# A transformer block with a routed self-attention on one core: work moved from VectorE to ScalarE, and orders redone around the routed attention and at the opening

## The chip, the cores and the metric

One NeuronCore of a Trainium2 chip runs the program; the other cores are not used. The metric is the device time of one execution in microseconds. The kernel before was timed three times: 2812.5, 2813.47 and 2815.11 us, median 2813.47.

## The reference

64 batches of x (256 tokens, 256 channels) and of a context (77 keys, 192 channels), fp32. First a cross-attention with 8 heads of 64, then a routed ("expert") self-attention with 16 experts; both with a layer norm in front and a residual.

```python
x = x + xattn(layernorm(x), ctx)          # q = x Wq, k = ctx Wk, v = ctx Wv, softmax, Wo, + bo
x = x + ffn(layernorm(x))

def ffn(h):
    logits = normalize(h) @ normalize(sim) - sigmoid(gates)     # 256 tokens x 16 experts
    mask = logits > 0, or the 2 best where none is
    rw = softmax(where(mask, relu(logits), -inf))
    q, k, v = [einsum("te,ted->td", rw, einsum("tc,ecd->ted", h, p)) for p in (q_proj, k_proj, v_proj)]
    a = softmax(causal(q k^T / 8)) v                            # one head of 64
    return einsum("ted,edc->tc", a[:, None, :] * rw[:, :, None], o_proj)
```

## The kernel before, in words

Each fp32 product is done as three products of a high and a low part (fp32r tiles `_hi` and `_lo`): `product` issues them in lines 467, 468 and 469. So whatever TensorE is to read is written twice: ScalarE evacuates the hi part from PSUM or SBUF, then VectorE the lo part as source minus hi.

The cross-attention is folded: for each group of three batches, "jobs" compute keys (`k`), values (`v`), and from them gq (key times Wq, 8 jobs `g`) and uo (value times Wo, 8 jobs `u`). These are written to DRAM through a two-slot buffer `draft` by SP and loaded back per batch, `gq` (1232 KB) by `load_g` and `uo` (1024 + 208 KB) by `load_u`. A batch then goes through these stages:

- A: `ln1_a` (statistics of x), the power on GpSimd, `ln1_b` (normalise to xn), `a_xT` (transpose), `a_s` (scores, four quarters, with the maxima L1163 on VectorE), `a_exp` (L893, 16 exponentials on ScalarE), `a_psum`, `a_p` (L1506, the softmax product on GpSimd), `a_pT` (transposes in three parts), `a_y` (product with uo; evacuation L1185 adds the residual and gives x2).
- B: `ln2_a`, power, `ln2_b` (x2n), `b_norm`, `b_xT` (L632), `b_qkv` 0 to 15: projections of 8 pairs of experts by 2 token tiles; `b_qkv(n, j)` has pair j // 2 and tile j % 2. Pair 0 brings the router's logits along; from these `b_top` and `b_index` on VectorE, `b_route_1`, `b_route_2`, `b_w` on GpSimd, `b_exp` on ScalarE, `b_wsum` on VectorE and `b_rw` on GpSimd (L1482) make the weights rw. Then VectorE evacuates every projection: pair 0 as `acc = bank * rw` (L1232, "opening"), the others as `acc += bank * rw` (L1235). `b_sum` on GpSimd (L1491) adds the two experts of a pair.
- C: `c_qk` (transpose q and k; four ScalarE and two VectorE pieces), `c_s` (scores, L666), `c_exp`, `c_p`, `c_pT`, `c_pv`, `c_mix` (attention times rw per expert, L1276, then L961 on ScalarE and L1511 on GpSimd), `c_y` (output product), store.

All engines run the same list of steps i = -2 to 65, each with an order written out by hand. In step i, `nxt` is batch i + 2 (ln1, a_xT), `ahead` batch i + 1 (rest of A), `now` batch i (ln2, b_xT, b_qkv 0 to 5), `before` batch i - 1 (b_qkv 6 to 15, then C up to the mix), `earlier` batch i - 2 (c_y). Between them stand the slots E0 to E3, M1 to M3, L1, L2, in which `turn` runs a key or value job. `JOBS[i % 3]` says which: kind 0 has g3 to g7, k3, v0, v1; kind 1 has u0 to u5, v2, v3 and ct (context transpose); kind 2 has u6 (E0), u7 (E1), k0, k1, g0, g1, k2, g2. In kind 2, SP also issues four context loads at the step's start, and `load_u` of the next batch right after the u7 store in E1; otherwise `load_u` stands behind M3. `load_x(i + 2)` and `load_g(i + 2)` stand behind E0's store on SP.

An engine executes its list in order, so a wait holds everything behind it. The projections go round three PSUM banks: `ring_b` (L505 to L513) makes fill f wait until fill f - 3 is evacuated, so `b_xT`'s second part waits for `b_qkv` 14 of the batch before. The cross-attention shares three other banks in the order `A_ORDER`; `freed` makes a slot wait for the last holder.

The opening: weights are loaded in 16 pieces through three staging areas and split into hi and lo (`split_weights`), at places that `SPLIT_AFTER` names; the first group's jobs run one after another. Pieces 6 to 13 are the expert projections, 14 and 15 o_proj.

## Time and profile before

| | |
|---|---|
| median of 3 runs | 2813.47 us |
| the profiled execution | 2814.86 us |
| its span, first to last instruction | 2813.1 us |
| mean granted TensorE clock, of full speed | 0.978 |
| busy: TensorE (matmul), VectorE, ScalarE, GpSimd | 90%, 78%, 49%, 39% |
| chain that ended last: TensorE, VectorE, ScalarE, issue, DMA | 59%, 19%, 12%, 7%, 2% |
| DMA queues: SP's (q1), ScalarE's (q10) | 374.15 MB, 68.17 MB |
| L1235 on VectorE, the later projection evacuations | x1792, 410 ns each, 659.7 us |
| L1276 on VectorE, the mix | x256, 906 ns each, 231.8 us |
| L1436 on GpSimd, the powers (two forms) | x128, 871 ns each, 111.4 us |
| L1136 on VectorE, keys and values lo | x352, 395 ns each, 139.2 us |

Busy times are unions of an engine's instructions. Matmuls are pipelined: one lasts 0.28 to 0.36 us by the profile, while the next starts 0.12 to 0.18 us later, so idle time before a matmul is a little shorter than what the wait cost. "Issue" is time in which the engine waited for nothing that the profile shows.

### The profile page before, as it was taken

Reading aid. Unit: us, or ns where it says so; the run is one execution under the profiler, and the core shown is the slowest. Engines: PE = TensorE matmul, PEld = TensorE weight load, DVE = VectorE, ACT = ScalarE, POOL = GpSimd, SP = SyncE. Lnnn points to the kernel's source line nnn. Section 1 sums busy time; section 2 is a strip of 40 time slices with the busy share of each in tenths; the row PEclk is TensorE's granted clock in tenths of the full one; section 3 lists DMA queues with packets and bytes.
Section 4 is the critical chain, followed back from the end, with each engine's and each line's share of the span. In section 5 each row is a group of like instructions: output and inputs, shape, how many; then the busy total and the mean of one; then the engine's idle time right before and its main releaser. Section 6 shows DMA issues by size and latency. Waiting matters only on the chain.

```text
span 2813.1 us, 53794 instructions
## 1 busy us (share of the span) xinstructions
PE 2528.2 (90%) x17308; PEld 2427.3 (86%) x17308; DVE 2201.7 (78%) x6491; ACT 1378.8 (49%) x4598; POOL 1103.9 (39%) x1611
## 2 busy tenths in 40 slices
PE   4599999999999899999999999999989999999987
PEld 3589889889889889889889989988989988988986
DVE  5488888888888777878878878888778888888874
ACT  4454454555455454455455545545445455545531
POOL 0134344434434434434434434433434433443442
PEclk6699999999999999999999999999999999999998
DMA  7555555464555455455555555465555446455531
GB/s 188 186 158 169 172 165 160 139 189 142 172 170 161 149 165 164 137 184 154 168 163 169 155 157 177 133 186 155 169 159 163 156 146 189 139 173 167 161 91 41
DMA packets 299936, 445.75 MB, mean 158 GB/s; under 512 B 36857, under 2 KB 210873, under 8 KB 291465
## 3 DMA queue, kind: packets, MB, share of 16 engines
q1 hardware_dynamic: 230024, 374.15, 41.5%
q10 hardware_dynamic: 69632, 68.17, 10.9%
q8 instruction: 140, 2.29, 0.3%
q14 instruction: 140, 1.14, 0.1%
HBM read 257.91 MB, written 184.35 MB: 157 GB/s over the span
## 4 chain that ended last, share of the span: by engine, by line
PE 59%; DVE 19%; ACT 12%; issue 7%; DMA 2%; POOL 1%; SPq 0%; DVEq 0%; ACTq 0%; POOLq 0%
PE bank_b L467 9%; PE bank_b L469 8%; PE bank_b L468 8%; DVE acc L1235 5%; PE bank_a L467 4%; PE bank_c L467 4%; PE bank_c L469 4%; PE bank_c L468 4%; PE bank_a L468 4%; PE bank_a L469 4%; DVE both L1136 2%; DVE pT_lo L1179 2%; DVE probs L1081 2%; ACT both L852 1%; ACT both L851 1%
## 5 line engine op out<-in xcount | busy, mean ns | idle before, releaser
L467 PE MATMUL bank_b<-wqkv_hi,x2T_lo 128*128 128x384 f32 (+1 forms) x2048 | 724.7, 354 | 18.4 <-DVE acc L1232 18.1
L1235 DVE SCALAR_TENSOR_TENSOR acc<-bank_b,rw,acc 128x192 f32<-128x192 f32 x1792 | 659.7, 410 | 61.5 <-PE bank_b L469 54.9
L469 PE MATMUL bank_b<-wqkv_hi,x2T_hi 128*128 128x384 f32 (+1 forms) x2048 | 692.2, 338 | 0.0
L468 PE MATMUL bank_b<-wqkv_lo,x2T_hi 128*128 128x384 f32 (+1 forms) x2048 | 690.8, 337 | 0.0
L1511 POOL TENSOR_TENSOR mixs_lo<-mix,mixs_hi 128x512 fp32r<-128x512 f32 x256 | 404.1, 1609 | 227.0 <-ACT mixs_hi L961 227.0
L893 ACT ACTIVATE probs<-bank_a,s_max 128x77 f32<-128x77 f32 x1024 | 317.3, 330 | 281.8 <-DVE s_max L1163 279.2
L467 PEld LDWEIGHTS bank_b<-wqkv_hi,x2T_lo 128*128 128x128 f32 x2048 | 386.6, 189 | 29.5 <-DVE acc L1232 26.8
L468 PEld LDWEIGHTS bank_b<-wqkv_lo,x2T_hi 128*128 128x128 f32 x2048 | 387.9, 189 | 0.0
L469 PEld LDWEIGHTS bank_b<-wqkv_hi,x2T_hi 128*128 128x128 f32 x2048 | 384.6, 188 | 0.0
L1506 POOL TENSOR_TENSOR probs<-probs,p_sum 128x616 f32<-128x616 f32 x128 | 155.8, 1217 | 356.9 <-DVE p_sum L1170 356.9
L467 PE MATMUL bank_c<-wo_hi,mixs_lo 128*128 128x256 f32 x1024 | 288.6, 282 | 3.7 <-POOL mixs_lo L1511 3.7
L1436 POOL TENSOR_TENSOR pow_out<-pow_in,expo 128x2 f32<-128x2 f32 (+1 forms) x128 | 111.4, 871 | 452.2 <-DVE pow_in L1073 315.9
L469 PE MATMUL bank_c<-wo_hi,mixs_hi 128*128 128x256 f32 x1024 | 288.1, 281 | 0.0
L468 PE MATMUL bank_c<-wo_lo,mixs_hi 128*128 128x256 f32 x1024 | 287.7, 281 | 0.0
L961 ACT ACTIVATE mixs_hi<-mix 128x512 fp32r<-128x512 f32 x256 | 161.7, 632 | 231.4 <-DVE mix L1276 231.4
L1136 DVE TENSOR_TENSOR both<-bank_a,only 64x231 fp32r<-64x231 f32 x352 | 139.2, 395 | 141.3 <-ACT both L852 139.0
L1276 DVE TENSOR_TENSOR mix<-rw_all,late_tiles 128x512 f32<-128x512 f32 x256 | 231.8, 906 | 2.2 <-ACT late_tiles L957 2.1
L893 ACT ACTIVATION_READ_ACCUMULATOR probs<-bank_a,s_max 128x1 f32 x1024 | 215.4, 210 | 0.0
L467 PE MATMUL bank_a<-uo,pT_lo 128*128 128x256 f32 (+1 forms) x640 | 189.2, 296 | 18.1 <-issue 17.9
L467 PEld LDWEIGHTS bank_c<-wo_hi,mixs_lo 128*128 128x128 f32 x1024 | 193.4, 189 | 4.1 <-issue 3.8
L468 PEld LDWEIGHTS bank_c<-wo_lo,mixs_hi 128*128 128x128 f32 x1024 | 194.2, 190 | 0.0
L469 PEld LDWEIGHTS bank_c<-wo_hi,mixs_hi 128*128 128x128 f32 x1024 | 193.5, 189 | 0.0
(204 smaller groups left out, 6161.7 us busy)
## 6 DMA issues: line engine op xcount, KB each, us to landing
g_dram<-draft SPq DMA_DIRECT2D x176, 462.0 KB
gq<-g_dram SPq DMA_DIRECT2D x64, 1232.0 KB, 5.5
uo<-u_dram SPq DMA_DIRECT2D x64, 1024.0 KB
rw_all<-rw_dram ACTq DMA_DIRECT2D x128, 512.0 KB, 7.4
u_dram<-draft SPq DMA_DIRECT2D x176, 308.0 KB
xt<-in_x_dram SPq DMA_DIRECT2D x64, 256.0 KB, 3.9
out_dram<-mix SPq DMA_DIRECT2D x64, 256.0 KB, 6.2
u_dram<-draft SPq DMA_DIRECT2D x88, 156.0 KB
```

The lines of the kernel that those rows point to most:

```text
L467: nc.tensor.matmul(dst, lhs[1], rhs[0], start=start, stop=False)
L468: nc.tensor.matmul(dst, lhs[0], rhs[1], start=False, stop=False)
L469: return nc.tensor.matmul(dst, lhs[0], rhs[0], start=False, stop=stop)
L893: last = nc.scalar.activation(probs[:, t, h * NC:(h + 1) * NC], bank_a(f"S{j}")[:, k * NC:(k + 1) * NC], ACT.Exp, bias=s_max[:, j, k:k + 1 ...
L961: nc.scalar.activation(mixs[0][:, 2 * j:2 * j + 2, :], mix[:, 2 * j:2 * j + 2, :], copy).then_inc(mix_hi, 1)
L1081: V.tensor_scalar(dst[:, t, :], src[:, t, :], mv[k][:, t, 0:1], pow_out[k][:, 0, t:t + 1], ALU.subtract, ALU.mult).then_inc(ln_done[k], 1)
L1136: last = V.tensor_tensor(both[rows, k, e, cols], src[rows, cols], only.bitcast(F32)[rows, k, e, cols], ALU.subtract)
L1235: V.scalar_tensor_tensor(acc[:, t, k, :], src, rw[:, t, e:e + 1], acc[:, t, k, :], ALU.mult, ALU.add).then_inc(b_evac, 1)
L1276: V.tensor_tensor(mix[:, 2 * j:2 * j + 2, :], rw_all[:, 2 * j:2 * j + 2, :], aT2[:, :].unsqueeze(1).to_broadcast([P, 2, T]), ALU.mult).the ...
L1436: G.tensor_tensor(dst, src, expo[:, 0:m], ALU.pow).then_inc(ln_pow[k], 1)
L1506: G.tensor_tensor(part, part, p_sum[:, half, 1, :, :].unsqueeze(3).to_broadcast([P, NT, HB, NC]), ALU.mult).then_inc(p_ready, 1)
L1511: G.tensor_tensor(mixs[1][:, 2 * j:2 * j + 2, :], mix[:, 2 * j:2 * j + 2, :], mixs[0].bitcast(F32)[:, 2 * j:2 * j + 2, :], ALU.subtract).t ...
```

## The change

- The projections' opening pieces (pair 0, both tiles) go from VectorE to ScalarE: `b_first(n, t)`, two scaled copies each, after a wait for rw. TensorE's and VectorE's waits follow with a semaphore of their own, `acc_opened`, and `b_read`'s count shrinks.
- `ln1_b` and `ln2_b` go from VectorE to ScalarE, as `Identity` with a scale and a bias. VectorE makes the negated mean (`minus`), GpSimd multiplies it with the power's result (`shift`).
- VectorE: ln1_a moves from E2 to E0, between `b_norm` 0 and 1; ln2_a behind the first maximum; `b_qkv` 12 ahead of the E2 job, 15 ahead of E3; `c_qk` ahead of the M2 job; `b_index` ahead of `c_s`; `b_wsum` and `a_y` ahead of `c_pT`; `b_qkv` 2 and 3 ahead of the mix.
- ScalarE: `c_qk` ahead of the M2 job.
- TensorE: `b_qkv` 2 ahead of `c_s`, `a_y` whole ahead of `c_pT`, `b_qkv` 3 ahead of `c_pv`.
- Opening: SP issues the first `load_g` and `load_u` before the steps; weight pieces 11 to 15 are split within step -1, and 14 and 15 loaded there; the first `ln1_b` stands on ScalarE behind the query weights.

```diff
@@ -88,7 +88,8 @@
     def b_read(n, fill):
-        return (B_QKV + 2 * NT * EP) * n + (fill + 1 if fill < B_QKV else 2 * fill)
+        assert not B_QKV <= fill < B_QKV + NT
+        return (B_QKV + 2 * NT * (EP - 1)) * n + (fill + 1 if fill < B_QKV else 2 * (fill - NT))
 
@@ -334,7 +339,7 @@
         SPLIT_AFTER = {("k", 1): (W_V,), ("k", 2): (W_O - 1, W_O), ("k", 3): (6,), ("v", 0): (7,), ("v", 1): (8,),
-                       ("u", 0): (9,), ("u", 2): (10,), ("u", 7): range(11, len(PIECES))}
+                       ("u", 0): (9,), ("u", 2): (10,)}
 
@@ -430,10 +435,14 @@
                     load_x(i + 2)
-                if on(i + 2):
+                if i == -1:
+                    load_weights((14,))
+                if on(i + 2) and i + 2 > 0:
                     load_g(i + 2)
+                if i == -1:
+                    load_weights((15,))
                 turn("E1")
-                if i % 3 == 2 and on(i + 1):
+                if i % 3 == 2 and on(i + 1) and i + 1 > 0:
                     load_u(i + 1)
@@ -451,10 +460,12 @@
                 load_weights(pieces)
-            for hc, pieces in enumerate(((12,), (13,), (), (14, 15))):
+            load_g(0)
+            for hc, pieces in enumerate(((12,), (13,), (), ())):
                 store_u(0, 2 * hc)
...
                 load_weights(pieces)
+            load_u(0)
             for i in range(-2, B + 2):
@@ -507,7 +518,9 @@
                 if n or fill >= B_BANKS:
-                    if fill >= B_BANKS:
+                    if B_QKV <= fill - B_BANKS < B_QKV + NT:
+                        pe.wait_ge(acc_opened, at(NT, n, fill - B_BANKS - B_QKV))
+                    elif fill >= B_BANKS:
                         pe.wait_ge(b_evac, b_read(n, fill - B_BANKS))
@@ -794,13 +807,13 @@
                 do(now, b_qkv, 1)
+                do(now, b_qkv, 2)
                 do(before, c_s)
-                do(now, b_qkv, 2)
                 fill("Y", ahead, a_y, 0)
+                do(ahead, a_y, 1)
                 do(before, c_pT)
-                do(ahead, a_y, 1)
+                do(now, b_qkv, 3)
                 do(before, c_pv)
-                do(now, b_qkv, 3)
                 do(now, b_qkv, 4)
@@ -912,6 +925,37 @@
 
+            def b_first(n, t):
+                act.wait_ge(rw_ready, at(1, n, 0))
+                act.wait_ge(b_fill, b_at(n, B_QKV + t))
+                if n == 0:
+                    act.wait_ge(sim_step, 5)
+                else:
+                    act.wait_ge(qkv_ready, at(NT, n - 1, t))
+                for e in range(2):
+                    last = nc.scalar.activation(acc[:, t, e, :], bank_b(B_QKV + t)[:, E + e * QKV:E + (e + 1) * QKV], copy,
+                                                scale=rw[:, t, e:e + 1])
+                last.then_inc(acc_opened, 1)
+
+            def ln_b(k, n, src, dst):
+                act.wait_ge(ln_shift[k], at(1, n, 0))
+                for t in range(NT):
+                    nc.scalar.activation(dst[:, t, :], src[:, t, :], ACT.Identity, bias=shift[k][:, t:t + 1],
+                                         scale=pow_out[k][:, 0, t:t + 1]).then_inc(ln_done[k], 1)
+
+            def ln1_b(n):
+                if n:
+                    act.wait_ge(xt_fill, at(1, n - 1, 0))
+                    act.wait_ge(pt_fill, at(3, n - 1, 2))
+                ln_b(0, n, xt, xn)
+
+            def ln2_b(n):
+                if n:
+                    act.wait_ge(b_fill, b_at(n - 1, B_XT + 1))
+                if n > 1:
+                    act.wait_ge(mix_lo, at(4, n - 2, 1))
+                ln_b(1, n, x2_tiles[n % 3], x2n)
+
             def c_part(n, fill, dst, src):
@@ -965,6 +1009,7 @@
                     query_weights()
+                    ln1_b(0)
                 elif kind == "k":
@@ -999,27 +1044,42 @@
                 do(before, c_rT)
+                if i == -1:
+                    split_weights(11)
                 do(ahead, a_exp, 0)
...
                 do(ahead, a_exp, 3)
+                if i == -1:
+                    split_weights(12)
+                do(now, ln2_b)
                 turn("E1")
...
                 do(ahead, a_pT, 2)
+                if i == -1:
+                    split_weights(13)
+                if nxt:
+                    do(nxt, ln1_b)
                 turn("E3")
...
                 do(nxt, a_xT)
+                if i == -1:
+                    split_weights(14)
+                do(before, c_qk)
                 turn("M2")
-                do(before, c_qk)
                 turn("M3")
+                if i == -1:
+                    split_weights(15)
                 do(before, c_exp)
                 do(now, b_exp)
+                do(now, b_first, 0)
                 do(before, c_pT)
+                do(now, b_first, 1)
                 do(before, c_pv)
@@ -1069,41 +1129,26 @@
                 dve.wait_ge(ln_stats[k], at(2 * NT, n, 2 * NT - 1))
+                if n:
+                    dve.wait_ge(ln_shift[k], at(1, n - 1, 0))
+                V.tensor_scalar(minus[k][:, :], mv[k][:, :, 0], -1.0, None, ALU.mult).then_inc(ln_var[k], 1)
                 if k == 0:
...
 
-            def ln_b(k, n, src, dst):
-                dve.wait_ge(ln_pow[k], at(1, n, 0))
-                for t in range(NT):
-                    V.tensor_scalar(dst[:, t, :], src[:, t, :], mv[k][:, t, 0:1], pow_out[k][:, 0, t:t + 1],
-                                    ALU.subtract, ALU.mult).then_inc(ln_done[k], 1)
-
...
             def b_norm(n, k):
                 if k == 0:
+                    dve.wait_ge(ln_pow[1], at(1, n, 0))
                     V.tensor_tensor(rn[:, 0, :], pow_out[1][:, 0, :], pow_out[1][:, 1, :], ALU.mult).then_inc(rn_step, 1)
@@ -1220,20 +1265,15 @@
                 dve.wait_ge(b_fill, b_at(n, fill))
-                if j == 0:
-                    dve.wait_ge(rw_ready, at(1, n, 0))
-                if ep == 0 and n:
-                    dve.wait_ge(qkv_ready, at(NT, n - 1, t))
                 for k in range(2):
                     e = 2 * ep + k
-                    lo = (E if ep == 0 else 0) + k * QKV
-                    src = bank_b(fill)[:, lo:lo + QKV]
-                    if ep == 0:
-                        V.tensor_scalar(acc[:, t, k, :], src, rw[:, t, e:e + 1], None, ALU.mult).then_inc(b_evac, 1)
+                    src = bank_b(fill)[:, k * QKV:(k + 1) * QKV]
+                    if ep == 1:
+                        dve.wait_ge(acc_opened, at(NT, n, t))
                     else:
                         dve.wait_ge(b_evac, b_read(n, fill - NT) - 1 + k)
-                        V.scalar_tensor_tensor(acc[:, t, k, :], src, rw[:, t, e:e + 1], acc[:, t, k, :],
-                                               ALU.mult, ALU.add).then_inc(b_evac, 1)
+                    V.scalar_tensor_tensor(acc[:, t, k, :], src, rw[:, t, e:e + 1], acc[:, t, k, :],
+                                           ALU.mult, ALU.add).then_inc(b_evac, 1)
 
@@ -1285,7 +1325,7 @@
                 def do(n, fn, *k):
-                    if on(n) and not (fn in (ln1_a, ln1_b) and n == 0):
+                    if on(n) and not (fn is ln1_a and n == 0):
                         fn(n, *k)
@@ -1305,56 +1345,62 @@
                 do(before, b_qkv, 7)
+                if i == -1:
+                    split_weights(11)
+                do(ahead, a_s, 0)
                 do(now, ln2_a)
-                do(ahead, a_s, 0)
                 do(before, b_qkv, 8)
                 do(ahead, a_s, 1)
-                do(now, ln2_b)
                 do(before, b_qkv, 9)
                 do(ahead, a_s, 2)
-                do(now, b_norm, 0)
                 do(before, b_qkv, 10)
-                do(now, b_norm, 1)
                 do(ahead, a_psum, 0)
                 do(ahead, a_s, 3)
+                do(now, b_norm, 0)
+                do(nxt, ln1_a)
+                do(now, b_norm, 1)
+                do(ahead, a_psum, 1)
                 do(now, b_norm, 2)
-                do(ahead, a_psum, 1)
                 do(before, b_qkv, 11)
+                if i == -1:
+                    split_weights(12)
                 turn("E1")
                 do(earlier, c_y)
+                do(before, b_qkv, 12)
                 turn("E2")
-                do(nxt, ln1_a)
-                do(before, b_qkv, 12)
                 do(ahead, a_pT, 0)
...
                 do(ahead, a_pT, 2)
-                do(nxt, ln1_b)
+                if i == -1:
+                    split_weights(13)
                 do(before, b_qkv, 14)
+                do(before, b_qkv, 15)
                 turn("E3")
-                do(before, b_qkv, 15)
                 do(now, b_xT, 0)
...
                 do(nxt, a_xT)
+                if i == -1:
+                    split_weights(14)
+                do(before, c_qk)
                 turn("M2")
-                do(before, c_qk)
                 do(now, b_top)
+                do(now, b_index)
+                if i == -1:
+                    split_weights(15)
                 do(before, c_s)
-                do(now, b_index)
                 do(before, c_p)
                 turn("M3")
+                do(now, b_wsum)
+                do(ahead, a_y)
                 do(before, c_pT)
-                do(now, b_wsum)
-                do(now, b_qkv, 0)
-                do(now, b_qkv, 1)
-                do(ahead, a_y)
+                do(now, b_qkv, 2)
+                do(now, b_qkv, 3)
                 do(before, c_mix, 0)
-                do(now, b_qkv, 2)
                 do(before, c_mix, 1)
-                do(now, b_qkv, 3)
+                do(now, b_qkv, 4)
                 do(before, c_mix, 2)
-                do(now, b_qkv, 4)
                 do(before, c_mix, 3)
@@ -1365,7 +1411,6 @@
             V.tensor_copy(sim_n[:, :], bank_b(0)[:, 0:E]).then_inc(sim_norm, 1)
-            ln1_b(0)
             split_weights(0)
@@ -1424,7 +1469,7 @@
             def power(n, k):
-                pool.wait_ge(ln_var[k], at(k + 1, n, k))
+                pool.wait_ge(ln_var[k], at(k + 2, n, k + 1))
                 m = (k + 1) * NT
@@ -1434,6 +1479,8 @@
                 G.tensor_tensor(dst, src, expo[:, 0:m], ALU.pow).then_inc(ln_pow[k], 1)
+                pool.wait_ge(ln_pow[k], at(1, n, 0))
+                G.tensor_tensor(shift[k][:, :], minus[k][:, :], pow_out[k][:, 0, :], ALU.mult).then_inc(ln_shift[k], 1)
 
```

## Rows read from the trace of the kernel before

**Rows 1.** Busy by stretch: length, PE, PEld, DVE, ACT, POOL, PEclk, DMA share, GB/s.

```profile
400.00:2600.00 2200.00, 2035.41 (x14136) 1960.66 (x14135) 1776.82 (x5281) 1111.39 (x3749) 901.53 (x1314) 1.00 0.54 162
```

**Rows 2.** Instructions of line 1185: duration min/median/max ns, first and last start.

```profile
L1185 DVE TENSOR_TENSOR x_first<-bank_a,xb x22: 678/681/692, 115.1 to 2732.6; 128x512 f32<-128x512 f32 x22
```

**Rows 3.** Waits, 380 to 2504 us: us in total, times, longest.

```profile
PE bank_c L666 <- DVE mixs_hi L1246: 47.9, 51, 1.5
...
PE bank_b L632 <- DVE acc L1235: 42.7, 50, 0.9
...
PE bank_a L467 <- issue: 12.9, 15, 2.5
```

**Rows 4.** Timeline of TensorE, a kind 1 step: start, us, what [idle before <-releaser].

```profile
1419.11 0.38 PE L577 MATMUL bank_a<-wo,both 128*116 128x256 f32 x1 [0.83 <-DVE pT_lo L1179]
...
1421.99 0.44 PE L632 MATMUL bank_b<-ident,mix 128*128 128x128 f32 x2 [0.89 <-DVE acc L1235]
...
1428.00 0.30 PE L666 MATMUL bank_c<-mixs_hi 128*128 128x128 f32 x1 [0.93 <-DVE mixs_hi L1246]
...
1434.55 0.44 PE L467 MATMUL bank_b<-wqkv_hi,x2T_lo 128*128 128x384 f32 x1 [0.27 <-DVE acc L1232]
```

**Rows 5.** Groups of instructions, whole span: count | busy us, mean ns | idle.

```profile
L1232 DVE TENSOR_SCALAR acc<-bank_b,rw 128x192 f32<-128x192 f32 x256 | 89.3, 411 | 26.7 <-POOL rw L1482 26.7
...
L1081 DVE TENSOR_SCALAR probs<-xt,mv,pow_out 128x256 f32<-128x256 f32 x128 | 46.7, 407 | 0.9 <-POOL pow_out L1436 0.9
...
L931 ACT ACTIVATE mix<-mix,m 128x256 f32<-128x256 f32 x64 | 31.6, 494 | 0.1
...
L819 ACT ACT_TABLE_LOAD x1 | 1.3, 1283 | 0.7 <-PEq L1557 0.7
```

**Rows 6.** Timeline of GpSimd, the router's chain of that step.

```profile
1428.78 0.23 POOL L1451 TENSOR_SCALAR z_top<-top 128x2 f32<-128x2 f32 x1 [3.51 <-DVE top L1204]
...
1431.88 0.25 POOL L1476 TENSOR_TENSOR w<-w,act_on 128x32 f32<-128x32 f32 x1
1433.41 0.24 POOL L1482 TENSOR_TENSOR rw<-w,w_sum 128x32 f32<-128x32 f32 x1 [1.29 <-DVE w_sum L1218]
```

**Rows 7.** Timeline of VectorE, ln1_a in that step.

```profile
1416.40 0.75 DVE L1066 BATCH_NORM_STATS2 stats<-xt 128x6 f32<-128x256 f32 x2
...
1417.72 0.74 DVE L1235 SCALAR_TENSOR_TENSOR acc<-bank_b,rw,acc 128x192 f32<-128x192 f32 x2
```

**Rows 8.** Timeline of ScalarE, the third pT piece.

```profile
1418.40 0.60 ACT L903 ACTIVATE pT_hi<-bank_a 128x512 fp32r<-128x512 f32 x1 [1.97 <-issue]
```

**Rows 9.** Timeline of SP: DMA issues, kind 1 and then kind 2 step.

```profile
1404.05 0.64 SPq L348 DMA_DIRECT2D xt<-in_x_dram  x1
...
1450.75 0.39 SPq L348 DMA_DIRECT2D xt<-in_x_dram  x1
...
1455.38 0.66 SPq L373 DMA_DIRECT2D u_dram<-draft  x2
1464.42 0.38 SPq L392 DMA_DIRECT2D uo<-u_dram  x1
```

**Rows 10.** DMA issues, us to landing: all x loads; issues at 1450.75 and 1451.25.

```profile
xt<-in_x_dram SPq DMA_DIRECT2D x64, 256.0 KB, 3.9
...
xt<-in_x_dram SPq DMA_DIRECT2D x1, 256.0 KB, 5.5
...
gq<-g_dram SPq DMA_DIRECT2D x1, 1232.0 KB, 7.9
```

**Rows 11.** Timeline of VectorE, fourth maximum of the kind 2 step.

```profile
1451.09 0.48 DVE L1163 TENSOR_REDUCE s_max<-bank_a 128x4 f32<-128x308 f32 x1
```

**Rows 12.** Timeline of TensorE, the product with uo in the kind 2 step.

```profile
1471.38 0.36 PE L467 MATMUL bank_a<-uo,pT_lo 128*128 128x256 f32 x1 [0.44 <-issue]
```

**Rows 13.** The chain that ended last, in the opening.

```profile
80.62 8.48 DMA mix<-in_L_ffn_o_proj_dram
```

**Rows 14.** Timeline of SP in the opening: the second batch's x load.

```profile
89.62 0.39 SPq L348 DMA_DIRECT2D xt<-in_x_dram  x1
```

15 lines of the change are left out of this document (4 added, 11 removed).

## Prediction

> **What bounds the kernel now.** I read the stretches first. Between 400 and 2600 us TensorE is busy 2035 of 2200 us at full clock, VectorE 1777, ScalarE 1111, GpSimd 902 [rows 1]. The evacuation of the cross-attention output starts once per batch, first at 115.1, last at 2732.6 [rows 2]: 63 intervals, 41.55 us each. So the time is an opening of 115, 63 steps, and a tail of 80. TensorE bounds the steps, but not without holes, and the waits say whose they are [rows 3]: over 51 steps the transposes of the routed part (L632) stand 50 times behind L1235, the scores (L666) 51 times behind L1246, and the product with uo 15 times behind "issue". The timeline of one step gives their size [rows 4]: idle 0.83, 0.89, 0.93 and 0.27 us, the last before projection 3, behind the router's weights. A pipelined matmul hides part of a wait, so each costs 0.1 to 0.2 more in spacing; together some 3.3 us of a step of 42. The reader should see that no single engine holds TensorE here: VectorE is late in the middle of the step, and at its end the router's chain is.
>
> I call a step by i mod 3, since the key and value work repeats in threes: the rows of 1416 to 1434 are of kind 1, those of 1450 to 1471 of kind 2.
>
> **The change, part by part.** *Load.* VectorE loses four normalising pieces at 0.407 us (L1081) and four opening pieces at 0.411 (L1232) [rows 5], eight pieces or 3.3 us a step, and gains two 128x2 negations, bounded by nothing and by L1232's 0.411; I take 0.2 each, being two columns. ScalarE gains eight pieces with a scale, four also with a bias, from 128x192 PSUM or 128x256 SBUF. No row shows that form; the bounds are VectorE's own 0.407 and, from ScalarE's exponential over 128x256 with one bias at 0.494, 0.1 more for the second operand, 0.6. I take 0.37 spacing for the 192 columns and 0.45 for the 256. The Trainium skill, ScalarE: Activation LUTs (What ACT_TABLE_LOAD costs), puts each per-partition operand at 93 ns over 186 + 0.833 ns per column, so 0.585 for a norm piece as an estimate; by it ScalarE's busy time would grow by some 0.5 us a step more, and the forecast by nothing, since no norm piece is on the chain. ScalarE is half idle, so only the pieces on a chain count. GpSimd gains two 128x2 products, bounded by 0.23 (L1451 in [rows 6]) and the power's mean of 0.87 in the profile's table; they fall in its idle time before and after the softmax products. ScalarE's ln2_b stands behind the 16 exponentials, where x2n is wanted 9 us later, and ln1_b behind the pT pieces.
>
> *Middle of the step (kinds 0 and 1).* Today ln1_a takes VectorE 1.32 us there (1416.40 to 1417.72 [rows 7]) and ln1_b about 0.7 more, ahead of the evacuations that TensorE waits for. Both go: ln1_a into an idle moment of E0, ln1_b to ScalarE. What is late next: ScalarE's third pT piece, which starts only at 1418.40 because two DMA issues stand before it [rows 8]. From there 0.60 + L1179 0.60 + one projection evacuation 0.65 gives the bank free at 1420.3; TensorE's second transposes move from 1421.99 to about 1420.35. Gain 1.6 us.
>
> *Scores.* c_qk's evacuation goes ahead of the M2 job on ScalarE and VectorE, and TensorE does projection 2 (1.05 us) before the scores. The hole of 0.93 closes. From the transposes at 1420.35, TensorE's jobs and transposes take 2.1 us as now, projections 0 to 2 with M3's job 3.85, the scores 0.55: the product with uo starts at 1426.85. Now it is 1429.6 (scores at 1428.00 [rows 4], then 0.55 and 1.05), so 2.7 earlier.
>
> *Router chain.* It now sets the pace: bank filled, scale and maximum, GpSimd, sum, rw, and new, two ScalarE pieces before projection 3 may start. Kind 1: projection 1 ends at 1425.35 by the shift above (now 1427.07, the last piece's start plus 0.34, in the same order); the M2 job's two pieces on VectorE (0.8) and b_top (0.7) put the maximum's end at 1427.2, and GpSimd starts 0.2 later. Its eleven operations, first 1428.78 and last 1431.88 + 0.25, take 3.35 us [rows 6]; then today b_wsum stands behind c_pT, and rw starts at 1433.41. Now b_wsum stands before it: 1427.4 + 3.35 + 0.9 for the rest of M3's evacuation, the sum and the reciprocal, + 0.25: rw is there at 1431.9. Two pieces of ScalarE, 0.75: projection 3 at 1432.65, where TensorE has been waiting since 1430.9. Behind ScalarE's wait for rw stand c_pT, the second opening piece, c_pv and the four mix copies. Today 1434.55. But c_pv (0.65 with its wait) now stands behind it, so projection 4 moves from 1435.60 to 1434.35. Of 2.7 us, 1.25 is left; for kind 0 the same steps give 1.2. After that TensorE has no hole in either order. 42 such steps: -51 us.
>
> *Kind 2, where I see a loss.* ln1_a now waits for the load of x in E0, with b_norm, the second softmax reciprocal, projection 11 and the u7 evacuation queued behind it on VectorE, and the softmax product, the transposes and SP's store behind those. In kinds 0 and 1 x is there: kind 1 issues it at 1404.05, the median landing is 3.9 us, and the fourth maximum comes near 1409. In kind 2 SP first issues four context loads: x is issued at 1450.75 and lands 5.5 later at 1456.2 [rows 9, 10], while VectorE is done with the fourth maximum at 1451.56 [rows 11]. SP's order is the same in every kind 2 step, so VectorE stands about 3.7 us in each (x may go out 0.5 earlier, since VectorE frees u5 sooner). TensorE loses about 1.4 at the transposes and 1.7 at the third ones. But TensorE waits later in this step anyhow: the load of uo needs the u7 store landed, issued 1455.38, load 1464.42, product at 1471.38 after 0.44 idle [rows 9, 12]. With the middle's gains TensorE would be there at about 1467.9, with the loss at 1469.6; so that is covered. Left is the store, issued 3.1 us later. It is issued while gq's 1232 KB, landing at 1459.2, are ahead of it in SP's queue [rows 10], and load_u follows that landing by 5.2; I take the store's delay as hidden up to 3.8 and add 0.8 for the rw_all loads, which slip by 2 us onto uo's. The Trainium skill, DMA: Bandwidth & Descriptors (Queues, rings and completion order), says an engine takes a queue's descriptors in ring order and a semaphore lands after the earlier writes; by it the whole 3.1 is hidden, and the store's part of the loss is 0. Behind the product the new order gives nothing here (c_pv behind projection 3 waits for its own evacuations). Kind 2: +0.8 (0 to 3.5), 21 steps: +17.
>
> *Opening.* Weight pieces 11 to 15 leave the stretch before the first scores, where o_proj's landing takes 8.48 us of the chain [rows 13]; the first gq and uo loads come before. VectorE would be 10 us earlier at the first maxima. But gq's load stands before the u stores in SP's queue, and these gate ScalarE through the draft buffers: +4 to 5 us. And load_x(1), now issued at 89.62 [rows 14], follows the wait for the last u store, the uo load and 6.5 us of context issues: about 95, landing near 100; ln1_a(1), ahead of the second reciprocal, waits for it. That reciprocal is at 100.5 now and at 100 to 102 then. The splits interleaved after it cost 1 to 2. I take +1 (-8 to +6). The tail has two or three holes of the same sort as the steps: -2 (-4 to 0).
>
> **Sum.** -51 + 17 + 1 - 2 = -35, against the profiled execution's 2814.86 (2813.1 plus 1.8 around it): 2780. The median shown is 1.4 lower. I forecast 2778.
>
> **The rivals.** *A, less is left over than the chain has* (the router's chain is shorter than I count, or VectorE's wait for x is shorter): each of 42 steps keeps 1.9 instead of 1.25 and kind 2 loses nothing: -80 - 2 = 2732 to 2750. For it: VectorE is free 3 us more, and b_top might start at once. Against: GpSimd's 3.35 us are untouched. *B, slower: the x wait in kind 2.* Its place is ln1_a on VectorE's queue, its price 4.6 us a step if the store's delay goes through to uo and to the product: 21 x 4.6 = 97: 2813 - 51 + 97 - 1 = 2858 at most; with 3.3 of it through, 2830. It decides from 2.5 us a kind 2 step on. For it: the landing is late in all of them. Against: the constant distance from gq's landing to load_u. *C, the gain is taken back in full:* the middle's gain is eaten by ScalarE's longer pieces (0.6 instead of 0.37 to 0.45, four of them on the chain, 0.7 a step), kind 2 at +1.5: -23 + 31: 2805 to 2822. *D, the change costs table loads:* one load of 1.28 us now [rows 5]. Were Identity outside the loaded set, four more a step, 5.1 us of ScalarE, 60 to 320 us in all. The Trainium skill, ScalarE: Activation LUTs (Table sets: the hidden batching unit), has identity in every set; no row here shows Identity beside Exp. I leave 1 in 100.
>
> **How the numbers follow.** Forecast (2758 to 2800) 0.55; A 0.22; B 0.10; C 0.12; D 0.01. What a measurement can tell here is 0.2%, 5.6 us. Faster: the forecast, A and 0.03 of C, 0.80; same: 0.07 of C; slower: B, D and 0.02 of C, 0.13. The range leaves out the far end of A and most of B: 2742 to 2820.
>
> **What would show it.** Right: TensorE's waits on L1235 before L632 and on L1246 before L666 nearly gone; a new wait of 1.5 us a step before projection 3, released by the ScalarE opening piece; in every third step VectorE idle 3 to 4 us before the layer norm's statistics, released by the x load, with the uo product still 6.5 to 8 us behind load_u; three batch intervals together 123.0 instead of 124.65. Wrong: load_u more than 1 us later in kind 2; a second ACT_TABLE_LOAD; the first y evacuation outside 107 to 121; TensorE waiting for mixs_lo in c_y, whose slack is about 1 us.

## The result, and the profile after

Before, the kernel took 2812.98 us (median of 4 runs, 2806.64 to 2815.11); after, 2862.35 us (4 runs, 2850.17 to 2864.47). The ratio is 1.017, with a 95% interval of 1.0137 to 1.0203: slower by 49 us, where 2778 and "faster" had been forecast. The profiled execution took 2861.3 us, its span is 2859.5.

The stretch between 400 and 2600 us, in the columns of [rows 1]:

```profile
400.00:2600.00 2200.00, 2028.17 (x13900) 1974.52 (x13899) 1712.18 (x4873) 1253.74 (x4089) 889.18 (x1391) 0.97 0.52 159
```

It holds 236 matmuls fewer than [rows 1], and TensorE's granted clock has gone from 1.00 to 0.97. VectorE is 65 us less busy, ScalarE 142 more: the load did move.

The waits of the steady part (us in total, times, longest), against [rows 3]:

```profile
PE bank_a L478 <- issue: 64.0, 16, 4.9
...
PE bank_b L478 <- ACT acc L936: 56.4, 33, 2.0
DVE stats L1126 <- DMA xt<-in_x_dram: 52.9, 17, 3.8
...
PE bank_a L611 <- POOL probs L1553: 27.0, 16, 2.2
...
PE bank_b L645 <- DVE acc L1275: 5.7, 16, 0.5
```

The old wait of the routed transposes (now L645) has shrunk from 42.7 to 5.7, and that of the scores is gone. The foreseen wait before projection 3 is there (L936, 1.7 us each), and so is VectorE's for x in every third step (3.1 us each). But the first row, the product with uo, was 12.9 us in 15 waits; it is now 64.0 in 16, 4.0 us each.

The intervals between the evacuations of the cross-attention output (first and last start here, as in [rows 2]) say where it went:

```profile
L1230 DVE TENSOR_TENSOR late_tiles<-bank_a,xb x42: 691/692/693, 142.6 to 2734.9; 128x512 f32<-128x512 f32 x42
L1230 DVE TENSOR_TENSOR x_first<-bank_a,xb x22: 691/692/693, 115.9 to 2778.0; 128x512 f32<-128x512 f32 x22
```

Apart from the opening, the three kinds of interval had means of 41.18, 42.05 and 42.33 us; they now have 39.02, 40.71 and 47.89. Two of three became faster, the third lost more than both gained. Here is one third step (i mod 3 = 2) in SP's timeline; [rows 9] show the same step before:

```profile
1480.66 0.51 SPq L353 DMA_DIRECT2D xt<-in_x_dram  x1
1481.28 0.69 SPq L388 DMA_DIRECT2D gq<-g_dram  x1
1489.07 0.66 SPq L378 DMA_DIRECT2D u_dram<-draft  x2
1496.54 0.38 SPq L397 DMA_DIRECT2D uo<-u_dram  x1
```

VectorE in the same step. It stands 3.79 us at the statistics, and the u7 evacuation (L1203, into draft), for which SP's store of 1489.07 waits, comes behind them and behind projection 11's:

```profile
1486.17 0.75 DVE L1126 BATCH_NORM_STATS2 stats<-xt 128x6 f32<-128x256 f32 x2 [3.79 <-DMA xt<-in_x_dram]
...
1487.71 0.74 DVE L1275 SCALAR_TENSOR_TENSOR acc<-bank_b,rw,acc 128x192 f32<-128x192 f32 x2
1488.36 0.68 DVE L1203 TENSOR_TENSOR draft<-bank_a,draft 116x512 fp32r<-116x512 f32 x1
```

From x's issue to the store it is 8.4 us, where [rows 9] have 4.6. And TensorE at the product with uo:

```profile
1501.56 0.28 PE L680 MATMUL bank_c<-mixs_hi,q_rows 128*128 128x256 f32 x1
1505.02 0.55 PE L478 MATMUL bank_a<-uo,pT_lo 128*128 128x256 f32 x1 [3.18 <-issue]
1505.37 0.41 PE L479 MATMUL bank_a<-uo,pT_hi 128*128 128x256 f32 x1
1505.58 0.41 PE L480 MATMUL bank_a<-uo,pT_hi 128*128 128x256 f32 x1
```

Two things are to be seen: 3.18 us idle, and then matmuls that follow each other at 0.21 us. The same 256-column matmuls run at 0.11 us in the other steps. Short stretches show why (columns as in [rows 1]; the granted clock is the figure behind GpSimd's busy time):

```profile
1501.90:1505.00 3.10, 0.00 (x0) 0.01 (x1) 1.98 (x13) 1.10 (x5) 2.46 (x10) 0.79 1.06 361
1505.00:1508.00 3.00, 2.98 (x14) 3.00 (x15) 0.35 (x2) 0.73 (x2) 0.65 (x3) 0.50 0.33 107
1508.00:1511.00 3.00, 3.00 (x17) 3.00 (x17) 0.00 (x0) 0.00 (x0) 0.00 (x0) 0.58 0.00 0
1511.00:1514.00 3.00, 2.77 (x20) 2.49 (x19) 2.46 (x6) 1.31 (x4) 0.00 (x0) 1.00 0.37 100
```

The clock falls within TensorE's idle time and the product begins at 0.50, 1.2 GHz; it is back at 2.4 GHz when most of the product is over. In the other two kinds of step TensorE's new idle time stands before projection 3. In this step, of kind 1, it is 1.72 us and the clock stays at 1.00:

```profile
1332.20:1334.20 2.00, 0.34 (x3) 0.10 (x1) 1.24 (x4) 0.73 (x3) 0.66 (x3) 1.00 0.36 104
1334.20:1337.00 2.80, 2.75 (x17) 2.75 (x18) 2.11 (x6) 1.39 (x5) 0.00 (x0) 1.00 0.32 104
```

In a later step of kind 1 it is 1.72 us again, and the clock falls (a line of TensorE's timeline, then a stretch):

```profile
1462.31 0.45 PE L478 MATMUL bank_b<-wqkv_hi,x2T_lo 128*128 128x384 f32 x1 [1.72 <-ACT acc L936]
1462.20:1465.20 3.00, 2.89 (x12) 2.89 (x13) 1.95 (x5) 1.06 (x4) 0.00 (x0) 0.59 0.28 92
```

Of the 33 such waits between 400 and 2560 us (1.67 to 1.95 us idle) nine end at the lower clock, eight of them among the 17 of kind 1. In those eight steps the stretch from the product to the next scores takes 24.53 us, in the other nine 22.99. In the kernel before, no step of kinds 0 and 1 shows the lower clock in that stretch.

To compare kernels I cut each step at two points of TensorE's order: the end of the fourth scores product (S3, in E0) and the start of the product with uo. Means over the 16 to 18 steps of each kind between 400 and 2560 us, in us, computed from the instructions' times in each trace; "slow" is how many of the product's first 29 matmul-to-matmul distances are above 0.15 us, mean over 20 third steps. Differences of up to 0.5 between kernels in one cell can come from single late steps. The kernel before was timed again beside every group of experiments, with medians of 2812.4 to 2814.0, so times from different groups can be compared; the ratios are to it.

```
                          ---------- third step ----------    other two steps
kernel            us      S3->uo  idle  slow  uo->S3  sum     kind 0  kind 1
before         2813.0     20.68   0.77   3.4  21.73  42.41    41.21   41.91
after          2862.4     23.28   3.97  20.6  23.50  46.78    39.84   41.23
1              2808.5     21.15   3.25  11.6  22.76  43.91    40.61   41.13
2              2818.8     21.17   4.24  23.6  23.92  45.09    39.79   41.09
3              2855.2     23.77   2.66  13.5  22.67  46.44    40.42   40.95
4              2815.7     23.46   0.39   0.9  21.56  45.02    39.86   40.94
5              2833.1     27.06   0.00   0.0  18.08  45.14    39.95   41.22
6              2820.0     20.61   3.69  23.3  23.81  44.42    39.91   41.14
7              2823.3     21.09   1.18   2.8  21.65  42.74    41.22   41.91
8              2895.9     23.60   4.14  19.3  24.31  47.91    40.95   40.73
9              2820.9     20.77   3.68  23.1  23.84  44.61    39.77   41.59
10             2807.7     20.35   0.44   2.0  21.59  41.94    41.21   41.88
11             2770.8     21.49   0.73   0.9  21.56  43.05    39.77   40.64
12             2859.5     23.50   3.75  19.6  23.44  46.94    39.97   41.00
13             2793.4     20.12   3.20  20.3  23.43  43.55    39.71   41.10
14             2776.2     21.02   2.17   1.8  21.68  42.70    39.66   40.69
15             2794.0     21.10   0.34   0.6  21.55  42.65    40.50   41.65
16             2759.7     19.97   0.33   1.0  21.56  41.53    39.92   41.16
17             2821.5     20.84   3.93  24.4  23.99  44.83    39.85   41.38
18             2709.2     17.79   0.88   2.5  21.92  39.71    39.92   40.52
```

The first two lines close the account: 21 times (-1.37 - 0.68 + 4.37) is +48.7 us, where +49.4 was measured. The third step's loss has two parts: 2.60 us between the scores and the product, 1.77 behind the product.

### The profile page after: what moved, and what is told of

Same layout as the page of the kernel before. It is cut to its first block, busy times and chain, and to the rows that moved or that the text cites. A ratio compares the mean times of both kernels' runs of the same rounds, so it can differ in the third digit from the quotient of the medians.

```text
span 2859.5 us, 54177 instructions
## 1 busy us (share of the span) xinstructions
PE 2559.7 (90%) x17308; PEld 2482.2 (87%) x17308; DVE 2158.7 (75%) x6107; ACT 1581.5 (55%) x5110; POOL 1105.5 (39%) x1739
## 3 DMA queue, kind: packets, MB, share of 16 engines
q10 hardware_dynamic: 69632, 68.17, 10.1%
## 4 chain that ended last, share of the span: by engine, by line
PE 62%; issue 11%; ACT 9%; POOL 7%; DVE 6%; ACTq 3%; DMA 2%; SPq 0%; POOLq 0%; DVEq 0%
PE bank_b L478 9%; PE bank_b L479 9%; PE bank_b L480 9%; PE bank_c L478 4%; PE bank_c L479 4%; PE bank_c L480 4%; PE bank_a L478 4%; PE bank_a L479 4%; PE bank_a L480 4%; ACTq L996 3%; POOL probs L1553 2%; PE bank_a L611 2%; PE bank_a L578 1%; DVE acc L1275 1%; DMA u_dram<-draft 1%
## 5 line engine op out<-in xcount | busy, mean ns | idle before, releaser
L478 PE MATMUL bank_b<-wqkv_hi,x2T_lo 128*128 128x384 f32 (+1 forms) x2048 | 732.1, 357 | 73.3 <-ACT acc L936 73.0
L479 PE MATMUL bank_b<-wqkv_lo,x2T_hi 128*128 128x384 f32 (+1 forms) x2048 | 698.0, 341 | 0.0
L1558 POOL TENSOR_TENSOR mixs_lo<-mix,mixs_hi 128x512 fp32r<-128x512 f32 x256 | 381.0, 1520 | 428.9 <-ACT mixs_hi L1005 428.9
L1316 DVE TENSOR_TENSOR mix<-rw_all,late_tiles 128x512 f32<-128x512 f32 x256 | 281.1, 1138 | 24.5 <-ACT late_tiles L1001 24.5
L478 PE MATMUL bank_a<-uo,pT_lo 128*128 128x256 f32 (+1 forms) x640 | 203.1, 317 | 83.4 <-issue 83.3
L1538 POOL TENSOR_TENSOR mix<-acc 128x192 f32<-128x192 f32 x128 | 76.3, 596 | 374.1 <-DVE acc L1275 373.0
L478 PEld LDWEIGHTS bank_a<-uo,pT_lo 128*128 128x128 f32 (+1 forms) x640 | 142.4, 223 | 87.4 <-issue 87.0
L479 PE MATMUL bank_a<-uo,pT_hi 128*128 128x256 f32 (+1 forms) x640 | 199.4, 312 | 0.0
L480 PE MATMUL bank_a<-uo,pT_hi 128*128 128x256 f32 (+1 forms) x640 | 198.1, 309 | 0.0
```

The costliest lines, as they stand in the source:

```text
L478: nc.tensor.matmul(dst, lhs[1], rhs[0], start=start, stop=False)
L479: nc.tensor.matmul(dst, lhs[0], rhs[1], start=False, stop=False)
L480: return nc.tensor.matmul(dst, lhs[0], rhs[0], start=False, stop=stop)
L1316: V.tensor_tensor(mix[:, 2 * j:2 * j + 2, :], rw_all[:, 2 * j:2 * j + 2, :], aT2[:, :].unsqueeze(1).to_broadcast([P, 2, T]), ALU.mult).the ...
L1538: G.tensor_tensor(qkv[:, t, :], acc[:, t, 0, :], acc[:, t, 1, :], ALU.add).then_inc(qkv_ready, 1)
L1558: G.tensor_tensor(mixs[1][:, 2 * j:2 * j + 2, :], mix[:, 2 * j:2 * j + 2, :], mixs[0].bitcast(F32)[:, 2 * j:2 * j + 2, :], ALU.subtract).t ...
```

## The experiments

**The questions.** Theory B: the wait for x delays u7's store, thereby uo, and the product's lateness costs the clock too. Rivals: the loss is ScalarE's longer pieces (C), the transfers as such (called D in the expectation of experiment 2; it is not the prediction's D), or a clock that falls for another reason. The prediction's D, more table loads, is out at once: the changed kernel has one ACT_TABLE_LOAD, as before.

**1. Statistics back at the head of E2**, on VectorE.

```diff
                 do(now, b_norm, 0)
-                do(nxt, ln1_a)
                 do(now, b_norm, 1)
...
                 turn("E2")
+                do(nxt, ln1_a)
```

> The changed kernel with one part undone: VectorE takes the first layer norm's statistics of the next x again at the head of E2, not in E0. Theory B (in every third step the statistics wait for x on VectorE, the u7 evacuation, its store and the uo load are queued behind them, and the uo product comes 3 to 4 us late and then runs at half clock): the third step falls from 48 to about 42 us, the idle time before the uo product to under 1.5 us, and the kernel takes 2735 to 2770 us, with 0 to 1.3 us a step lost again in the other two. Rival C (the loss comes from the longer ScalarE pieces and the new TensorE order, and the wait for x only sits beside it): the third step stays above 46 us and the kernel at 2845 to 2880. Rival K (the clock falls for another reason than this wait): the granted clock in the product stays at half in most third steps.

2808.46 us, ratio to the kernel before 0.9975 (0.9962 to 0.9988). The third step falls by 2.9 us and the chain from S3 to the product by 2.1, back to about what it was. So C is out as the main cause. But the time is 38 us or more above what B gave, for TensorE still idles 3.25 us before the product and the clock still falls in 12 of 17 third steps: the waits that the change removed elsewhere in that step have only gathered there. All the rest of the change together is worth 4 us, where I had counted on a gain of some 50.

**2. x ahead of the context loads.**

```diff
+                early = i % 3 == 2 and i // 3 + 3 < GROUPS and on(i + 2) and i > 0
+                if early:
+                    load_x(i + 2)
                 if i % 3 == 2 and i // 3 + 3 < GROUPS:
                     load_ctx(i // 3 + 3)
```

> The changed kernel with one thing altered on SyncE's queue: in every third step x is issued ahead of the four context loads instead of behind them; VectorE's order stays as changed. Theory B: x is there before VectorE asks for it, the third step falls to 41 to 42.5 us, the other two stay at 39.0 and 40.7, in all 2725 to 2745. Rival C: the third step stays above 46. Rival D (what makes the uo load late is SyncE's and the DMA engines' load of transfers as such, not the wait for x): u7's store goes out earlier but the uo load still 7 us or more behind gq's landing, the product starts less than 1.5 us earlier, 2830 to 2850.

2818.77 us, 1.0012 (0.9996 to 1.0028). VectorE has its x, u7's store goes out 4.5 us ahead of gq's landing instead of with it, the chain is 2.1 us shorter, again 21.2. As in experiment 1 the time between is lost at the product: 4.24 us idle and 23.6 slow matmuls. B's number was again some 80 us too low. What it says of the chain held (the load is 4.6 us behind gq's landing and the product 2.1 us earlier, which is against D); that the step would shrink to 42.5 us or less did not (45.09).

**3. That one move in the kernel before.**

```diff
                 do(ahead, a_s, 3)
+                do(nxt, ln1_a)
                 do(now, b_norm, 2)
...
                 turn("E2")
-                do(nxt, ln1_a)
```

> The kernel before with one part of the change alone: the statistics of the next x move from the head of E2 to E0 on VectorE, everything else as before. Theory B: this one move carries the whole loss: third steps grow from 42.1 to 46 to 48.5 us, the other two gain 0 to 1.3 us each, in all 2830 to 2930. Rival C: the wait is hidden as it was, within 10 us of the kernel before.

2855.17 us, 1.0139 (1.0118 to 1.0161). Its place on VectorE alone makes the kernel 43 us slower:

```profile
DVE stats L1066 <- DMA xt<-in_x_dram: 72.6, 17, 5.0
...
PE bank_a L467 <- issue: 43.2, 16, 3.8
```

The other two kinds of step gain 0.8 and 1.0 us from it, the third loses 4.0.

**4. Work for TensorE in the wait.**

```diff
                 if t == 0:
+                    if n and n % 3 == 0:
+                        for k in range(34):
+                            nc.tensor.matmul(bank_a("Y")[:, 0:C], x2T[0][:, 0, 0:P],
+                                             wqkv[0][:, 0, E:E + C], start=True, stop=True)
                     pe.wait_ge(u_in, 32 * (n + 1))
```

> The changed kernel with 34 extra products on TensorE ahead of its wait for uo in every third step; they write the bank that the uo product starts anew, so the results do not depend on them. They take about 3.6 us of the 4.1 us in which TensorE idles there. Theory K (the idle time itself makes the clock fall to half for the following 14 to 27 matmuls, 1.5 to 2.9 us a third step): with TensorE at work the clock stays up, the uo product runs at 0.107 us a matmul and the kernel is 30 to 60 us faster than the changed one, about 2810 to 2830, though no wait is shorter. Rival (the clock falls for another reason, such as the load on the chip): the same slow matmuls, 2860 to 2875.

2815.73 us, 47 us less than the changed kernel, by 34 matmuls more in every third step. The chain is as long as there (23.46), the slow matmuls are gone, and the time from the product to the next scores falls from 23.50 to 21.56. So the clock's fall is an effect of the idle time, and it is a cost of its own, about 1.9 us a third step, or 41 us. The other 6 us are in kind 1, where 5 of 17 steps met the lower clock and not 8.

**5. The product behind projection 4 in third steps** (with x first; VectorE's `a_y` behind `b_qkv` 4 likewise).

```diff
+                third = i % 3 == 2 and i > 0
+                if not third:
+                    fill("Y", ahead, a_y, 0)
+                    do(ahead, a_y, 1)
                 do(before, c_pT)
                 do(now, b_qkv, 3)
                 do(before, c_pv)
                 do(now, b_qkv, 4)
+                if third:
+                    fill("Y", ahead, a_y, 0)
+                    do(ahead, a_y, 1)
```

> The changed kernel with x issued ahead of the context loads in every third step, and in those steps the uo product and its evacuation put behind projection 4 (TensorE: scores, c_pT, projection 3, c_pv, projection 4, then the product), so that TensorE has work of its own while uo lands. The theory, with the accounts of the runs so far: from the third scores product of the step to the uo product 21.2 us pass whatever TensorE does (gq 8.0 to 8.6, its landing to the uo load 4.6 to 5.1, the load to the product 7.5); the changed kernel waits idle there for about 4 us and then pays 1.2 to 2.2 of clock. With 2.7 us of work moved ahead of the product and no slow matmuls, third steps fall from 45.1 (x first alone) to about 40.5, the kernel to 2715 to 2745. Rival (the router's chain, not the load, is what TensorE stands at in these steps too, and the product only changes places with it): idle time before projection 3 of 2 to 4 us, third steps 43 to 45, 2780 to 2815.

2833.1 us, 1.0064: a miss, beyond even the rival's range. The wait for uo has gone from the list, and two others have come:

```profile
PE bank_b L481 <- ACT acc L944: 81.7, 50, 2.0
...
PE bank_c L690 <- DVE mix L1317: 51.7, 17, 3.6
```

The second one is the softmax of the routed attention, 3.0 us that the uo product hides in the other orders; then comes the router's chain. So the work put into the wait was not ready by then.

**6 and 7. gq behind the uo load**, in the changed kernel with x first (6) and in the kernel before (7).

```diff
+                late = i % 3 == 2 and i > 0 and on(i + 2)
-                if on(i + 2) and i + 2 > 0:
+                if on(i + 2) and i + 2 > 0 and not late:
                     load_g(i + 2)
...
                     load_u(i + 1)
+                if late:
+                    load_g(i + 2)
```

> The changed kernel with x issued ahead of the context loads in every third step, and in those steps the load of gq (wanted only in the next step) issued behind the u7 store and the uo load. The theory (load_u stands behind gq's 8 us of transfer): uo lands 5 to 8 us earlier, the idle time before the product goes from 4.2 to under 0.5 us, the product runs at 0.107 us a matmul, from the third scores product to the uo product 17 to 18 us pass as in the other steps; third steps about 40.5 to 41.5, in all 2715 to 2745. Rival (the wait is for the store's landing and the DMA engines' load, whatever the order): the wait stays above 2 us and the kernel above 2780.

> The kernel before with gq issued behind the u7 store and the uo load in every third step, nothing else. The theory: the loads were only just in time there (0.77 us idle before the product on average), so the kernel gains 0.5 to 1.0 us a third step, 10 to 20 us in all: 2790 to 2803. Rival (the idle time there is TensorE's own and not the load's): 2808 to 2815.

2820.0 us, 1.0026 (1.001 to 1.0043), and 2823.3 us, 1.0031 (1.0021 to 1.0041). In 6 the theory failed and its rival came true (idle 3.69 us, above 2780); in 7 the time lies above both ranges. In 6 the uo load goes out 2.9 us earlier after S3 than in 2 (10.7 instead of 13.6), but the product follows it after 9.9 us and not 7.5. What is gained ahead of the load is lost behind it. But most of that is not gq's doing: in experiments 13 and 10 below, the load goes out as early (10.7 and 10.9) with gq landed before it, and the product still follows after 9.4 and 9.5 us. Against these, gq behind the load adds 0.5 us in 6 and 0.8 in 7.

**8. The opening pair back on VectorE** (the first lines are ScalarE's, the last VectorE's).

```diff
-                do(now, b_first, 0)
                 do(before, c_pT)
-                do(now, b_first, 1)
...
+                do(now, b_first, 0)
                 do(before, c_pT)
+                do(now, b_first, 1)
```

> The changed kernel with one part undone: VectorE scales the four opening pieces again (0.41 us each), in front of and behind its part of c_pT; ScalarE keeps the norms; the orders stay as changed. If the router's chain up to the weights sets projection 3 (theory), the wait before it stays at about 2 us and the other two steps of three lengthen only by what VectorE has to do more, 0 to 0.8 us each, 2865 to 2895. If ScalarE's place behind its exponential and its wait is what holds projection 3 (rival), the wait shrinks by 0.5 us or more and the kernel is faster than the changed one by 10 to 30 us.

2895.93 us, 1.0283: 0.9 us above the theory's range. The wait before projection 3 stays (77.4 us in 48 times, 1.6 each), the three steps together are 1.7 us longer. The loss lies otherwise than expected, in kinds 0 and 2 (1.1 us each), while kind 1 gains 0.5: the lower clock has moved from 8 of 17 steps of kind 1 to 10 of 16 of kind 0. Of the parts undone alone, ScalarE's opening pieces are the one that gains: 34 us.

**9 and 10. Context loads behind the last uo load**, in the changed kernel (9) and in the one before (10).

```diff
-                if i % 3 == 2 and i // 3 + 3 < GROUPS:
+                ctx = i % 3 == 2 and i // 3 + 3 < GROUPS
+                if ctx and i < 0:
                     load_ctx(i // 3 + 3)
...
                 if i % 3 != 1 and on(i + 2):
                     load_u(i + 2)
+                if ctx and i > 0:
+                    load_ctx(i // 3 + 3)
```

> The changed kernel with the four context loads of every third step moved on SyncE's queue from the head of the step to behind its last uo load; they are read two steps later. Theory (in third steps everything from the third scores product to the uo product is a chain of transfers: 8 us for gq where the other steps have 5.5, then the u7 store and uo, and what sits ahead of them on the queue stretches it): x and the u6 store go out about 5 us earlier, gq takes 5.5 to 6.5 us, VectorE no longer waits for x, the span from the scores to the uo product falls from 23.3 to 18 to 19.5 us, the idle time to 1 to 2 us, and the slow matmuls go: third steps 46.8 to about 41, in all 2725 to 2750. Rival (the chain is as long without them, since the store's landing and uo's 1.2 MB are its body): 21 us as with x first alone, idle time 3.5 to 4.5 us, 2800 to 2820.

> The kernel before with the four context loads moved in the same way and nothing else. There TensorE idles only 0.77 us on average before the third step's uo product, so by the theory little is to be had: 0.5 to 1.0 us a third step, 2793 to 2806. Rival (the loads slow something else in that step): more than 1.5 us a third step, below 2785, or no gain at all, 2808 to 2816.

2820.9 us, 1.0023 (1.0012 to 1.0033): the rival's account (20.8 us, 3.68 idle), 0.9 us above its range. gq takes 5.7 us instead of 7.5, yet x still stood behind the u6 stores and VectorE waited for it 11.9 us in 16 times, so this run did not part the two. In the kernel before, 2807.65 us, 0.9978 (0.9968 to 0.9987): a gain of 0.5 us a third step. The time lies between the two ranges, 1.7 us above the theory's.

**11. x first, and the wait filled.** Edits 2 and 4 together.

> The changed kernel with x issued ahead of the context loads and with the 34 extra products on TensorE ahead of its wait for uo in third steps. The idle time of 4.2 us with x first and the clock's price of 2.2 us behind it were measured apart; if they are two separate costs the second goes and the first stays: 2819 less 21 times 2.0 to 2.2, 2768 to 2778, with the granted clock near 1.0 between 400 and 2600 us. Rival (in the earlier filled run it was the late x that the fillers helped with): no more than 10 us below 2819.

2770.79 us, 0.985 (0.9833 to 0.9866), as expected. The two costs, the chain's and the clock's, are separate ones. The product in its trace, behind 1.25 us of idle time:

```profile
1452.16 0.39 PE L481 MATMUL bank_a<-uo,pT_lo 128*128 128x256 f32 x1 [1.25 <-DMA uo<-u_dram]
1452.38 0.28 PE L482 MATMUL bank_a<-uo,pT_hi 128*128 128x256 f32 x1
1452.50 0.28 PE L483 MATMUL bank_a<-uo,pT_hi 128*128 128x256 f32 x1
```

**12. Both norms' pieces back on VectorE**, at their old places (the first lines are ScalarE's, the others VectorE's).

```diff
-                do(now, ln2_b)
...
-                if nxt:
-                    do(nxt, ln1_b)
...
                 do(ahead, a_s, 1)
+                do(now, ln2_b)
...
+                if nxt:
+                    do(nxt, ln1_b)
                 do(before, b_qkv, 14)
```

> The changed kernel with one part undone: both layer norms' normalising pieces on VectorE again (four of 0.41 us a step), at the places they had; the opening pair stays on ScalarE and the orders as changed. By the prediction's step for the middle, the second transposes then wait longer and 0.7 us or more comes back in each of the steps of kinds 0 and 1, little in the third: 2885 to 2910. Rival (the pieces were in VectorE's slack and the gain is all from the orders and the opening pair): within 6 us of the changed kernel, 2856 to 2868.

2859.47 us, 1.0165: the rival's number. Moving 1.6 us a step off VectorE changed the time by 3 us. Yet it is not without effect: without it the product starts 0.2 to 0.4 us later in the other two steps, and from there to the next scores the steps at full clock take as long as in the changed kernel (23.04 and 22.97 us, against 23.04 and 22.99). What gives it back is the clock: it is low in 1 of 33 such steps and not in 9. Why it falls less often there was not tried.

**13. Both: x at the head of the step, context loads late.** Edit 9, with `load_x(i + 2)` of third steps ahead of `turn("E0")`.

> The changed kernel with, in every third step, x issued at the head of the step, ahead of the u6 stores, and the context loads behind the last uo load. If SyncE's queue stretches the chain (theory): VectorE finds x landed, u7's store goes out 4.5 us after the third scores product, gq takes 5.6, the uo load goes 10.5 to 11.5 us after the scores product and the uo product starts 18.5 to 19.5 us after it, idle 1.5 to 2.5 us, few slow matmuls: 2740 to 2770. If the transfers' own length is the body of the chain (rival): 20.5 to 21 us and idle 3.5 to 4.5 as with either move alone, 2805 to 2820.

2793.36 us, 0.9924 (0.9902 to 0.9947), between the two. u7's store goes out early and the uo load at 10.7 us after S3, as the theory said. But the product follows 9.4 us later instead of 7.5. In this run it starts 3.3 us or more behind the landing of the two rw_all loads (mean 3.9; 3.6 in the changed kernel), which stand ahead of uo on another queue; in every other kernel of the table but 18 it is at least 3.2 us.

**14. Half the filling.** Experiment 11 with 17 matmuls.

> The run with x first and 34 extra products, with 17 of them: TensorE idles some 2.4 us before the uo product in third steps instead of 0.7 (34 products) or 4.2 (none). TensorE idles 2.0 us before projection 3 in the other steps with no slow matmuls behind it, so theory: no or few slow matmuls, within 8 us of the run with 34, 2768 to 2779. Rival (the price grows evenly with the idle time): half of the 48 us between those two comes back, 2790 to 2800.

2776.2 us, 0.9881 (0.9858 to 0.9904): as expected, within 6 us of 11. With 2.17 us of idle time on average only one of 20 products was slow, while with none filled (experiment 2, idle 3.0 to 5.9 us) all 20 were. The price is not even in the idle time. But the expectation's premise, no slow matmuls behind the 2.0 us before projection 3, is not so, as shown above; and the idle time alone does not decide. Here the clock stayed up behind 3.18 us of it, and in experiment 3 it fell behind 1.91 and 1.94.

**15. Statistics late, and the wait filled with 26.** Edits 1 and 4.

> The changed kernel with the statistics back at the head of E2 and 26 extra products (2.8 us) ahead of the wait for uo in third steps, where it idled 3.25 us. Theory: only the clock's price goes, 1.2 us a third step: 2808 less 25, 2778 to 2788. Rival (fillers win more than that, since they also cover records of a slow clock elsewhere): below 2770.

2793.99 us, 0.993 (0.9913 to 0.9947), 6 us above the expectation. The third step falls by 1.26 us as expected, while kind 1 is 0.5 longer than in experiment 1. That is the clock again: behind the wait before projection 3 it is low in 6 of 16 steps of kind 1, in experiment 1 in none of 16, and such a step is 1.6 us longer. At which steps it falls stays open.

**16. Experiment 13 with 24 matmuls in the wait.**

> The changed kernel with x issued at the head of third steps, the context loads behind the last uo load, and 24 extra products (2.6 us) ahead of TensorE's wait for uo there. Without the products that order took 2793.4 us, idle 3.2 us and with 2.2 us of slow matmuls behind it. Theory: the clock's price goes, 21 times 2.0: 2748 to 2760. Rival (order and products do not add): above 2765, no better than x first with products, 2771.

2759.74 us, 0.9808 (0.9795 to 0.9821), at the upper end of the theory's range: order and filling add.

**17. Experiment 13 with gq behind uo.**

> As the run with x at the head and the context loads late (2793.4 us), with gq's load issued behind the uo load in third steps. If gq holds uo up: the span from the scores to the uo product falls from 20.1 to 17 to 18.5 us and the kernel to 2735 to 2765. If the rw_all loads do: the product stays 3.4 us or more behind their landing, the span stays at 19.5 to 20.5 us, 2785 to 2800.

2821.48 us, 1.0026: above both ranges. The uo load goes out 10.7 us after S3, exactly as in 13 where gq's 1232 KB stood ahead of u7's store. So with the context loads late gq does not hold the store up at all; behind the uo load it holds uo up by 0.7 us (10.1 to the product, 9.4 in 13), and the kernel is 28 us slower than 13. The product stays 4.4 us behind the landing of the rw_all loads, as that side of the expectation had it.

**18. Experiment 13 with the rw_all loads behind uo**, in third steps, on SP's queue (`c_rw` of ScalarE, and SP's step; `load_rw` issues the same two loads after the same waits).

```diff
+                if n > 1 and n % 3 == 1:
+                    return
                 for k in range(2):
...
                 if i % 3 == 2 and on(i + 1) and i + 1 > 0:
                     load_u(i + 1)
+                if i > 2 and i % 3 == 2 and on(i - 1):
+                    load_rw(i - 1)
```

> As the run with x at the head and the context loads late (2793.4 us), with the two rw_all loads of third steps issued on SyncE's queue behind the uo load, not on ScalarE's queue ahead of it. If they hold uo up: from the uo load's issue to the product 5 to 7 us instead of 9.4, the span from the scores to the uo product 16.7 to 18 us, hardly any idle time or slow matmuls, 2725 to 2755, unless VectorE then waits for rw_all at its mixes (0 to 2 us a third step more). If gq does: 9 us as now, 2785 to 2800.

2709.15 us (2706.05 to 2710.5), 0.9625 (0.961 to 0.964): 104 us faster than the kernel before and 153 than the changed one, with no filling. It is 16 us below the expected range. From the uo load to the product it is 7.2 us, the idle time is 0.88, and the clock stays up in 17 of 18 third steps; in kind 1 it is low in 1 of 17, in 13 in 7. Of the 2.3 us by which the chain is shorter than in 13, 2.2 lie behind the uo load. The edit changes two things at once, the place behind uo and the queue, and takes two issues off ScalarE; no run parts them. SP's timeline of one third step:

```profile
1516.43 0.39 SPq L353 DMA_DIRECT2D xt<-in_x_dram  x1
1516.87 2.40 SPq L378 DMA_DIRECT2D u_dram<-draft  x2
1522.82 0.35 SPq L388 DMA_DIRECT2D gq<-g_dram  x1
1527.03 0.64 SPq L378 DMA_DIRECT2D u_dram<-draft  x2
1533.24 0.38 SPq L397 DMA_DIRECT2D uo<-u_dram  x1
1533.66 0.47 SPq L399 DMA_DIRECT2D uo<-u_dram  x1
1534.23 1.41 SPq L410 DMA_DIRECT2D rw_all<-rw_dram  x2
```

And the product in it:

```profile
1539.92 0.36 PE L493 MATMUL bank_a<-uo,pT_lo 128*128 128x256 f32 x1 [0.28 <-issue]
1540.12 0.28 PE L494 MATMUL bank_a<-uo,pT_hi 128*128 128x256 f32 x1
```

The steady stretch's row answers to [rows 1], with 629 matmuls more in the same 2200 us:

```profile
400.00:2600.00 2200.00, 2100.88 (x14765) 2050.50 (x14764) 1816.41 (x5174) 1329.21 (x4326) 944.50 (x1483) 1.00 0.56 168
```

## Why the prediction was wrong

**The steps that held.** The first sign of being right, the waits before L632 and L666 nearly gone, came true, and so did the next two. The product started 2.7 us earlier by the forecast; from S3 to it, kinds 0 and 1 take 2.95 and 2.96 us less. Projection 3's new wait was put at 1.5 us or a little more; it is 1.7. The gain of kind 0 was put at 1.2 and is 1.37. For kind 1 it was 1.25 and is 0.68. In all that is -43 us of the -51. The chain itself gave more than forecast: the steps of kind 1 that keep the full clock take 40.51 us, a gain of 1.40, and the eight that lose it behind the new wait 42.05. Kind 1's shortfall is thus the clock's price, of which the prediction has nothing. The opening's +1 came out at +0.8 (115.9 against 115.1), and the tail, 81.5 against 80.4 us, at +1.1, where -2 was expected. VectorE's wait for x was put at 3.7 us in every third step; it is there, 3.1. Two of the sums are loose: from projection 1's end at 1425.35 the pieces of 0.8 and 0.7 give 1426.85, and 1427.2 is written; and that end itself is 1425.43 by the shift. ScalarE's norm piece was taken at 0.45 and its opening piece at 0.37 spacing:

```profile
L936 ACT ACTIVATE acc<-bank_b,rw 128x192 f32<-128x192 f32 x256 | 94.0, 424 | 145.9 <-POOL rw L1529 145.9
...
L943 ACT ACTIVATE probs<-xt,shift,pow_out 128x256 f32<-128x256 f32 x128 | 69.3, 591 | 0.0
```

The opening piece lasts 0.424 and the norm piece 0.591; two in a row start 0.32 and 0.49 apart. The Trainium skill, ScalarE: Activation LUTs (What ACT_TABLE_LOAD costs), gave 0.585 for the norm piece; the trace agrees. It changes the time little: with all norm pieces on VectorE (experiment 12) the kernel takes 2859.5.

**The step that failed** is kind 2: "I take the store's delay as hidden up to 3.8 and add 0.8 for the rw_all loads", +0.8 a step with 0 to 3.5. It measured +4.37, in two terms. Two of its own signs of being wrong came: load_u went out 1.56 us later after S3, and the product stood 8.6 us behind it, not 6.5 to 8.

The first is the chain, +2.60. The constant distance of 5.2 us from gq's landing to the uo load, the argument against rival B, held only while u7's store left 3.5 us ahead of that landing. The store was put 3.1 us later, and after S3 it is 3.04 later; gq lands 0.4 earlier, so the store now leaves as gq lands, and load_u follows 7.0 us behind the landing where it was 5.1. "Hidden up to 3.8" was the error: 1.56 of the 3.04 went through. From the store to the uo load it is 6.2 us even with no gq ahead (experiment 17), and it was 8.5 in the kernel before, so at most 2.3 us of delay could be hidden and not 3.8. The Trainium skill, DMA: Bandwidth & Descriptors (Queues, rings and completion order), had been read as hiding all of it. That reading fails here: the store was issued when gq had just landed, and no order on the queue could hide it. Then come 1.04 us by which uo itself is slower, put at 0.8: the rw_all loads, which stand behind the pT pieces on ScalarE, also go out 1.7 us later (8.44 after S3, where it was 6.72) and land 3.4 later. How the 2.60 divides between the store and these loads is my sum; experiments 1 and 2 undo both delays at once.

The second is the clock, +1.8 to 1.9 (experiment 4 against the changed kernel), of which the prediction has nothing. It said that in this step TensorE "would be there at about 1467.9, with the loss at 1469.6; so that is covered". Covered meant free, and it is not: moving TensorE's arrival forward in front of a fixed landing turned 0.8 us of idle time into 4.0, and with it most of the following product ran at 1.2 GHz. The granted clock of 1.00 in [rows 1] was itself a property of an order without long holes. The Trainium skill, TensorE: Matmul & The Clock Gate (What's actually happening), has the array's clock gated down when it has been idle; the rows at 0.50 agree. With kind 1's share (0.7 us a step, 15 in all) the clock took over 50 us.

**The rivals.** B was the right one and had 0.10. Its mechanism, place and sign are as written; its price of 4.6 a step is near the 4.37, but 2.6 of that is its own and the rest the clock's. Its range ended at 2858, 4 us short. The weight was wrong: what spoke for B was in every third step's rows, what spoke against it was one constant seen under one order of events. Experiment 3 shows that with this single move the kernel before is 43 us slower, and experiment 1 that all the rest is worth 4 us. The forecast's gain for the rest also took for granted that third steps would keep theirs. C had the pieces' length right (0.591) but its place wrong: the middle's gain stayed. A counted on more left over in the middle, and with the full clock 1.40 was left in kind 1, not 1.9.

## What to carry to other kernels

Where an engine waits for a load whose time is set by a chain of transfers, whatever brings it there sooner is lost; and on TensorE it may cost more than nothing, so look at the spacing of the matmuls behind every new wait, in each kind of step and over many steps: one step shown at full clock says little of the others. Follow such a load back through both queues: once x and the context loads were out of its way, two 512 KB loads for a later use, on another engine's queue, still held it up by some 2 us, and issuing them behind it was worth 84 us with what the clock gave back. Before an instruction with a DMA wait is moved up in an engine's order, read for every kind of step, not for the median, when its data lands, and count what stands behind it.

## What the runs showed of the hardware

- **The clock.** TensorE's granted clock fell to half, 1.2 GHz, behind idle times of 3.1 to 4.9 us before the product (19 of 20 in the changed kernel), and the 14 to 28 matmuls after it ran 0.21 us apart. It also fell behind some of the shorter ones: 9 of 33 waits of 1.67 to 1.95 us before projection 3, each for some 1.5 us more in its step. With 2.17 us of idle time on average before the product (experiment 14) it fell once in 20. 34 products whose results nobody reads made the kernel 47 us faster.
- **A later load on the same queue costs the earlier one little.** With gq (1232 KB) issued 0.5 us behind uo, uo took 9.9, 10.3 and 10.1 us to the product (6, 7, 17). With uo issued as early and gq not behind it, it took 9.4 (13) and 9.5 (10).
- **An earlier load on another queue costs more.** With the two rw_all loads (512 KB each) ahead on ScalarE's queue, uo took 9.4 us from issue to product (13); with them behind it on SP's, 7.2 (18).
- **Not ahead, though.** gq ahead of u7's store did not delay the uo load (10.7 us after S3 in both 13 and 17), nor did the context loads alone (10.7 in 6); the two together did (13.6 in experiment 2).
- **VectorE beside others.** VectorE's mix product of 128x512, the same instruction 256 times, went from a mean of 906 ns to 1138 (281.1 us in all). The first two of each batch take 0.69 us in both kernels; the last two take 1.13 before, and 1.4 or 1.8 after. GpSimd is at work during the whole of the last two in both kernels, and during 1% of the first two after the change. That its traffic slows them was not tried.
